# Two 3x3 convolution stages rewritten: strips of rows as 32x32 array tiles, a residual tap, statistics taken inside the stage

## The reference

```python
def _gn(v, G=16, eps=1e-5):
    ...
    m = jnp.mean(g, axis=(2, 3, 4), keepdims=True)
    s = jnp.var(g, axis=(2, 3, 4), keepdims=True)
    return ((g - m) / jnp.sqrt(s + eps)).reshape(v.shape)
...
# layer 1, first steps: 18 offset channels of which the kernel uses 10
offset = conv2d(input, offset_conv_w, offset_conv_b, padding=[(1, 1), (1, 1)])
offset = jnp.tanh(group_norm(offset, gn_offset_w, gn_offset_b, K))
...
# layer 2
out = jax.lax.conv_general_dilated(x, weight, ..., padding=((1, 1), (1, 1)))
return out + bias[None, :, None, None]
...
x = x + _L2_conv_ref(_gn(x), L2_conv_weight, L2_conv_bias)
x = x + _L3_conv_ref(_gn(x), ...)
```

## Time and profile before

| | |
|---|---|
| median of 3 runs | 25470.23 us (25365.6 to 25509.12) |
| profiled execution, first to last instruction | 25493.9 us |
| stage `l1o` in it (first transfer to the next stage's) | 797.4 us |
| stage `n1o` | 76.9 us |
| stage `l2` | 884.2 us |
| stage `n3` (to the first work of the next) | 125.9 us |
| TensorE busy in `l1o`, in `l2` | 365.4 us, 364.8 us |

### The profile page before, as it was taken

One profiled execution on the slowest core, in us unless ns is written; L12 is line 12 of the kernel. 1 busy time (PEld: TensorE's weight loads), 2 busy tenths in 40 slices (PEclk: granted clock), 3 DMA queues, 4 the chain that ended last, 5 costly groups with the idle time before them and its releaser, 6 DMA issues. The chain is left out here.

```text
span 25493.9 us, 384771 instructions
## 1 busy us (share of the span) xinstructions
PE 20717.4 (81%) x134800; PEld 8220.3 (32%) x134800; DVE 15361.5 (60%) x15737; ACT 14120.3 (55%) x22694; POOL 9395.5 (37%) x7816
## 2 busy tenths in 40 slices
PE   6888888884368888888859999997348888888899
PEld 2333333331122222222225444454013333333344
DVE  8999999994167777777835555555133333333111
ACT  6999998994257777777636665665222222222111
POOL 6777777782057777777720010001000000000000
PEclk9999999997678888888877776777679999999999
DMA  1000000006810000000031111112960011001111
GB/s 63 12 12 12 12 12 12 12 12 127 155 47 17 17 18 16 18 18 16 16 79 26 28 33 28 26 28 62 193 149 22 22 29 26 22 22 27 39 38 44
DMA packets 1295345, 995.42 MB, mean 39 GB/s; under 512 B 742248, under 2 KB 1151440, under 8 KB 1258968
## 3 DMA queue, kind: packets, MB, share of 16 engines
q1 hardware_dynamic: 1193416, 849.62, 15.9%
q0 software_dynamic: 26624, 100.67, 1.4%
q10 hardware_dynamic: 74448, 33.14, 0.5%
HBM read 771.60 MB, written 211.63 MB: 39 GB/s over the span
## 5 line engine op out<-in xcount | busy, mean ns | idle before, releaser
L270 DVE TENSOR_TENSOR l_mx<-l_p_v,l_puN 128x2048 f32<-128x2048 f32 x2560 | 5635.2, 2281 | 137.0 <-PE l_p_s L485 124.5
L485 PE MATMUL l_p_s<-l_mx,l_w2z 128*32 128x512 f32 x32768 | 3815.3, 610 | 579.5 <-ACT l_mx L397 307.9
L290 POOL TENSOR_TENSOR l_mx<-l_pv,l_puP 128x2048 f32<-128x2048 f32 x1024 | 3715.5, 3644 | 312.8 <-PE l_p_s L485 307.0
L1196 POOL TENSOR_TENSOR l1m_hc<-l1m_hs,l1m_cs 128x512 f32<-128x512 f32 x2304 | 2923.9, 1269 | 8.5 <-DVE l1m_hs L1148 8.1
L2072 PE MATMUL l3a_p<-l3a_xn,l3a_w 128*128 128x512 f32 (+1 forms) x6144 | 2682.9, 600 | 266.2 <-ACT l3a_xn L1963 266.2
L1148 DVE TENSOR_TENSOR_SCAN l1m_hs<-l1m_da,l1m_carry,l1m_pu 128x512 f32<-128x512 f32 x2304 | 2824.1, 1268 | 106.1 <-ACT l1m_da L1066 2.2
L2178 POOL DMA_DIRECT2D l3b_xt<-x_after x64 | 33.9, 529 | 7634.9 <-DVE l3b_most L2307 5811.9
L1790 ACT ACTIVATE l1d_ab<-l1d_pt 128x1024 f32<-128x1024 f32 x2304 | 2316.1, 1023 | 671.3 <-PE l1d_pt L1552 327.7
L416 ACT ACTIVATE l_mx<-l_pv,l_puP 128x128 f32<-128x128 f32 x8192 | 2446.7, 393 | 0.8
L1668 DVE TENSOR_SCALAR l1d_hat<-l1d_ab 128x1024 f32<-128x1024 f32 x2304 | 1917.0, 833 | 474.0 <-ACT l1d_ab L1790 363.6
L1587 PE MATMUL l1d_po<-l1d_hat,l1d_ring 128*32 128x128 f32 x36864 | 1893.2, 335 | 325.2 <-DVE l1d_hat L1668 214.1
(11 more groups left out here) (300 smaller groups left out, 27330.4 us busy)
## 6 DMA issues: line engine op xcount, KB each, us to landing
n_xt<-x_after SPq DMA_DIRECT2D x48, 2048.0 KB
l3a_xb<-x_after SPq DMA_DIRECT2D x352, 256.0 KB, 4.0
l1o_img<-x_after SPq DMA_DIRECT2D x32, 2032.0 KB, 17.5
l_img<-x_after SPq DMA_DIRECT2D x32, 2032.0 KB, 16.9
l1m_sq<-seq SPq DMA_DIRECT2D x256, 144.0 KB
n_xt<-in_x_dram SPq DMA_DIRECT2D x16, 2048.0 KB
l_xs<-in_x_dram SPq DMA_DIRECT2D x128, 256.0 KB, 2.8
x_after<-l_ot SPq DMA_DIRECT2D x128, 256.0 KB, 2.4
```

Source lines behind the costliest of these rows:

```text
L270: v.tensor_tensor(mx[:, r % QB, :, :, :], columns.unsqueeze(1).broadcast_to([P, 4, G, P]), rows.broadcast_to([P, 4, G, P]), ALU.max).then_ ...
L290: g.tensor_tensor(mx[:, r % QB, :, :, :], pv[:, u, :, :].unsqueeze(1).broadcast_to([P, 4, G, P]), rows.broadcast_to([P, 4, G, P]), ALU.add ...
L485: ins = pe.matmul(p_s[R * q:R * (q + 1), 512 * u:512 * (u + 1)], w2z[:, 31 - r:63 - r], mx[:, r % QB, q, :, :].rearrange("p t v -> p (t v) ...
L1196: g.tensor_tensor(hc[:, (3 * u + p) % 6, part, :], hs[:, p % 3, part, :], cs[:, u, :], ALU.mult).then_inc(hc_done, 1)
```

## The change

Both calls of `conv_layer` get a new body, and the two `norm_table` calls behind them (`n1o`, `n3`) go; the stage writes their tables itself. Lines L547 to L696 below are those of the changed kernel.

An image is cut into four strips of 32 rows. Strip s lies with its 32 channels in partitions 32 s to 32 s + 31 of `raw`, with one row more above and below, and is loaded once; the rows that belong to two strips are loaded twice. Loads go out on GpSimd's queue, stores on SyncE's. ScalarE normalises from `raw` into the padded `img` with one activation over 128 partitions and 4096 elements and four small ones for the border rows. A strip's 32 rows are four sub-strips k of 8 rows; a pass r (two for an image) makes four rows of each sub-strip. TensorE does, for each pass and each of nine taps, sixteen products, one on each 32x32 tile of the array: row tile s reads strip s, column tile k makes sub-strip k, and the result goes to bank 4 r + s. In `l2` a tenth tap with an identity matrix adds the unnormalised `raw`. An image takes 288 products in `l1o` and 320 in `l2`; the loop over images is written out for TensorE. ScalarE evacuates four banks at once with the bias. VectorE takes statistics of what was evacuated, and at the stage's end a product with `mean_strips` joins them over strips and channel pairs into the table. The scale and bias of all images are loaded once at the start.

```diff
--- before.py
+++ after.py
...
-def conv_layer(nc, stage, x, table, weights, bias, out, B, residual):
+def conv_layer(nc, stage, x, table, weights, bias, one, mix, out, out_table, B, residual):
...
+    S = 4
+    SR = H // S
+    SUB = SR // S
     RR = 512 // W
...
+    RN = SUB // RR
...
+        raw = m.sb("raw", [P, 2, SR + 2, W])
+        img = m.sb("img", [P, 2, SR + 2, WP])
...
+        ot = m.sb("ot", [P, 2, S, SUB, W])
...
+        acc = m.bank("acc", 2 * S)
...
+        @block.gpsimd
+        def _(g):
+            def load(b, u):
+                for s in range(S):
...
+                    g.dma_start(raw[strip(s), u, first:first + hi - lo, :],
+                                x[at(b), :, lo:hi, :].rearrange("b c h w -> (b c) h w")).then_inc(img_in[u], 16)
+            load(0, 0)
+            load(1, 1)
+            with g.Fori(0, B // 2 - 1) as j:
+                for u in range(2):
+                    g.wait_ge(norm_done, j * 2 + u + 1)
+                    if residual:
+                        g.wait_ge(conv_done, (j * 2 + u) * RN + 3 * RN)
+                    load(j * 2 + u + 2, u)
         @block.sync
         def _(sp):
...
+            tb = table.rearrange("b (c q) s -> c b q s", c=C)
+            for s in range(S):
+                sp.dma_start(gn[strip(s), :, :], tb[:, :, 0, :]).then_inc(w_in, 16)
...
+            for s in range(S):
...
             def store(b, u):
...
+                sp.wait_ge(evac_done, b * RN + 3 * RN)
+                for k in range(S):
+                    sp.dma_start(out[at(b)].rearrange("b c (s k r) w -> k (b c) s (r w)", s=S, k=S)[k],
+                                 ot[C * k:C * k + keep, u].rearrange("p s r w -> p s (r w)")).then_inc(stored[u], 16)
+            with sp.Fori(0, B // 2) as j:
                 for u in range(2):
                     store(j * 2 + u, u)
...
+            sp.wait_ge(tab_ready, 2)
+            sp.dma_start(out_table.rearrange("b (c q) s -> c b q s", q=q)[:, :, 0, :], tab[0:keep, :, :]).then_inc(tab_out, 16)
+            sp.wait_ge(tab_out, 16)
             for u in range(2):
                 sp.wait_ge(stored[u], (B // 2 + 1) * 64)
         @block.scalar
         def _(act):
...
+            act.wait_ge(w_in, 16 * n_w)
+            act.wait_ge(zeroed, 2)
+            def normalise(b, j, u):
+                act.wait_ge(img_in[u], j * 64 + 64)
+                act.wait_ge(conv_done, b * RN + RN)
+                def norm(part, rows):
+                    return act.activation(img[part, u, rows, 1:W + 1], raw[part, u, rows, :], ACT.Identity,
+                                          scale=gn[part, at(b), 0:1].rearrange("p b s -> p (b s)"), bias=gn[part, at(b), 1:2].rearrange("p b s -> p (b s)"))
+                norm(slice(C, 2 * C), slice(0, 1))
+                norm(slice(2 * C, P), slice(0, 1))
+                norm(slice(0, 2 * C), slice(SR + 1, SR + 2))
+                norm(slice(2 * C, 3 * C), slice(SR + 1, SR + 2))
+                norm(slice(0, P), slice(1, SR + 1)).then_inc(norm_done, 1)
+            def evacuate(b, j, u):
+                act.wait_ge(stored[u], j * 64 + 64)
+                act.wait_ge(stat_done, b * RN + RN)
+                for r in range(RN):
+                    act.wait_ge(conv_done, b * RN + (2 * RN + r + 1))
+                    act.activation(ot[:, u, :, RR * r:RR * (r + 1), :].rearrange("p s r w -> p s (r w)"),
+                                   acc[:, 512 * S * r:512 * S * (r + 1)].rearrange("p (s n) -> p s n", s=S),
+                                   ACT.Identity, bias=bc[:, 0:1]).then_inc(evac_done, 1)
+            normalise(0, 0, 0)
+            with act.Fori(0, B // 2 - 1) as j:
+                normalise(j * 2 + 1, j, 1)
+                evacuate(j * 2, j, 0)
+                normalise(j * 2 + 2, j + 1, 0)
+                evacuate(j * 2 + 1, j, 1)
+            normalise(B - 1, B // 2 - 1, 1)
+            evacuate(B - 2, B // 2 - 1, 0)
+            evacuate(B - 1, B // 2 - 1, 1)
...
         @block.tensor
         def _(pe):
...
+            pe.wait_ge(w_in, 16 * n_w)
+            taps = [(dy, dx) for dy in range(3) for dx in range(3)]
+            for j in range(B // 2):
                 for u in range(2):
...
+                    pe.wait_ge(norm_done, j * 2 + (u + 1))
+                    for r in range(RN):
+                        pe.wait_ge(evac_done, j * 2 * RN + (u * RN + r + RN + 1))
+                        for n, (dy, dx) in enumerate(taps):
+                            for s in range(S):
+                                for k in range(S):
+                                    r0 = SUB * k + RR * r + dy
+                                    ins = pe.matmul(acc[strip(k), 512 * (S * r + s):512 * (S * r + s + 1)], wt[strip(s), n, :],
+                                                    img[strip(s), u, r0:r0 + RR, dx:dx + W], start=n == 0,
+                                                    stop=n == len(taps) - 1 and not residual, tile_position=(C * s, C * k))
+                        if residual:
+                            for s in range(S):
+                                for k in range(S):
+                                    r0 = SUB * k + RR * r + 1
+                                    ins = pe.matmul(acc[strip(k), 512 * (S * r + s):512 * (S * r + s + 1)], idn[strip(s), :],
+                                                    raw[strip(s), u, r0:r0 + RR, :], start=False, stop=True, tile_position=(C * s, C * k))
                         ins.then_inc(conv_done, 1)
+            pe.wait_ge(mv_ready, 1)
+            pe.wait_ge(evac_done, B * RN + 2 * RN)
+            pe.matmul(acc[:, 0:2 * B], mx[:, :], mv[:, :, :].rearrange("p b s -> p (b s)"), start=True, stop=True).then_inc(mean_done, 1)
         @block.vector
         def _(v):
...
+                    for r in range(RN):
+                        v.wait_ge(evac_done, j * 2 * RN + (u * RN + r + 1 + 2 * RN))
+                        for s in range(S):
+                            ins = v.bn_stats(parts[:, at(j * 2 + u), S * r + s, :].rearrange("p b s -> p (b s)"),
+                                             ot[:, u, s, RR * r:RR * (r + 1), :].rearrange("p r w -> p (r w)"))
+                        ins.then_inc(stat_done, 1)
+            v.wait_ge(stat_done, B * RN + 2 * RN)
...
-    conv_layer(nc, "l1o", x1, tables[1], a["w_offset"], a["b_offset"], offsets, B, False)
-    norm_table(nc, "n1o", offsets, tables[2], a["pair_mean_half"], B)
+    conv_layer(nc, "l1o", x1, tables[1], a["w_offset"], a["b_offset"], a["one_strips"], a["mean_strips"], offsets, tables[2], B, False)
...
-    conv_layer(nc, "l2", x2, tables[3], a["w_l2"], a["b_l2"], x3, B, True)
+    conv_layer(nc, "l2", x2, tables[3], a["w_l2"], a["b_l2"], a["one_strips"], a["mean_strips"], x3, tables[4], B, True)
...
-    norm_table(nc, "n3", x3, tables[4], a["pair_mean"], B)
...
+def strip_conv(w):
...
+    o, i = w.shape[:2]
+    out = np.zeros((T, 9, T), np.float32)
+    out[:i, :, :o] = w.transpose(1, 2, 3, 0).reshape(i, 9, o)
+    return np.tile(out, (P // T, 1, 1))
...
+        mean_strips=np.tile(pair_means(2)[:T, :T], (P // T, P // T)) * (T / P), step_table=step_table, own_term=own_term, ident=one,
...
+        w_offset=strip_conv(I[L1 + "offset_conv_w"][:used]), b_offset=b_offset,
...
+        w_l2=strip_conv(I["L2_conv_weight"]), b_l2=I["L2_conv_bias"], b_conv1=I["L3_conv_conv1_b"],
```

More of the change, by code:

```diff
@@ L529, in _ @@
         @block.sync
         def _(sp):
[L531 to L547, removed]
@@ L549, in store @@
-            def store(b, u):
-                sp.wait_ge(evac_done, b * NS + 2 * NS)
-                for q in range(4):
-                    sp.dma_start(out[at(b), :, QR * q:QR * (q + 1), :].rearrange("b c h w -> (b c) (h w)"),
-                                 ot[C * q:C * q + keep, u, :]).then_inc(stored[u], 16)
-            load(0, 0)
-            load(1, 1)
-            with sp.Fori(0, B // 2 - 1) as j:
+            tb = table.rearrange("b (c q) s -> c b q s", c=C)
+            for s in range(S):
+                sp.dma_start(gn[strip(s), :, :], tb[:, :, 0, :]).then_inc(w_in, 16)
@@ L559, in _ @@
+            with sp.Fori(0, B // 2) as j:
                 for u in range(2):
                     store(j * 2 + u, u)
-                    load(j * 2 + u + 2, u)
-            for u in range(2):
-                store(B - 2 + u, u)
+            sp.wait_ge(tab_ready, 2)
+            sp.dma_start(out_table.rearrange("b (c q) s -> c b q s", q=q)[:, :, 0, :], tab[0:keep, :, :]).then_inc(tab_out, 16)
+            sp.wait_ge(tab_out, 16)
             for u in range(2):
@@ L607, in _ @@
-            v.memset(ot[:, 0, 2:3], 0.0).then_inc(stored[0], 64)
-            v.memset(ot[:, 1, 0:1], 0.0).then_inc(stored[1], 64)
-            v.wait_ge(w_in, 80)
+            for u in range(2):
+                v.memset(img[:, u], 0.0).then_inc(zeroed, 1)
+            v.memset(eps[:, :], EPS).then_inc(evac_done, 2 * RN)
+            v.memset(var[:, :], 0.0).then_inc(conv_done, 2 * RN)
```

(11 more changed lines are left out.)

92 lines of the change are left out of this document (41 added, 51 removed).

## The result

The changed kernel takes 24,515.8 us (median of 4 runs, 24,447.0 to 24,667.6) beside 25,468.9 us before (median of 4): 953 us less, and the two medians divide to 0.9626. The ratio on record, which goes by fast runs alone, is 0.9656, 95% interval 0.9612 to 0.9700, or 876 us. I had said 24,250 us and at most 24,520, against 25,470 a ratio of 0.952 and at most 0.963: the sign is right, the gain is about three quarters of the forecast, the median lies 4 us inside the end of the range, and the ratio on record just outside.

The account below looks back on a forecast made before the run. Transfers were taken to fill `l1o` and `l2`, slowed by using few partitions. New stages of 293 and 368 us sum to 661 against 1884.4, 1223 us less: 24,271 of 25493.9, adjusted to 24,250 us; range 24,120 to 24,520.

Parts of the forecast that it names:

- The feeding of TensorE: Both stages: sixteen pairs of weight load and pass issue in 0.43 us, 27 ns a pair, as a short run suggested.
- the rival that named it: Both stages: the sequencer sets the pace, up to 89 ns a pair, 2.85 us for sixteen products, total 25,400 us; chance 0.06.
- Sixteen products in 0.86 us: TensorE in both stages: two passes at 0.43 us; 15.5 us an image in `l1o`, 17.2 in `l2`.
- rows and columns overlap: TensorE in both stages: row and column tiles work at once, the lower bound of 0.86 us for sixteen products, against 3.44.
- row tiles in turn: Rival, both stages: row tiles take turns, sixteen products in 3.44 us, stages 2176 us, total 25,760 us; chance 0.05.
- half the rate: Rival, both stages: sixteen products in 1.72 us, by paired row tiles or low clock, total 24,715 us; chance 0.10.
- The chain of two images in `l2`: `l2`: load beside store, normalise, evacuation, products, hand-overs and clock follow each other, 41.0 us for two images, 20.5 an image.
- The start: Each stage: 15 us to the first normalisation, parameters and first load landing together, then 6.1 us to normalise.
- The end: Each stage: 3 us for the clock, 1.9 for the last evacuation, 17 for last statistics, table and barrier.
- Transfers: Both stages: a load takes 10.1 us and mostly overlaps stores, 11.7 us an image in `l1o`, 11.5 in `l2`.
- The tables: Separate stages `n1o` and `n3` go, saving 76.9 + 125.9 us; their statistics run beside other work.

Follow-up runs that it names:

- e5: Changed kernel with TensorE's loop body one image, passes making half the columns from padded buffers: `l1o` 370 us, `l2` 408 us, total 24,362 us.
- e2: Changed kernel loading only the first two images, the other fourteen reusing their strips: `l1o` 375 us, `l2` 402 us, total 24,288 us.
- e4: Changed kernel with row strips multiplied one after the other, four column tiles at a time: `l1o` 1583 us, `l2` 1701 us, total 26,815 us.
- e9: One-image loop with parameters first, each product on 256 columns for 512, half the output rows left out: `l1o` 263 us, `l2` 285 us, total 23,961 us.
- e3: Changed kernel with each strip loaded in pieces of at most 9 rows, packets of 4.6 KB: `l1o` 431 us, `l2` 473 us, total 24,546 us.
- e6: One-image loop, with GpSimd waiting for the stage's parameters before loading the first image: `l1o` 362 us, `l2` 402 us, total 24,298 us.
- e1: Changed kernel with TensorE's written-out stream made a loop over pairs of images: `l1o` 521 us, `l2` 521 us, total 24,843 us.

## Why the prediction was right in sign and wrong in size

The stages were to take 661 us and take 941.5; the difference is made of these (with e5's images as those without a fetch; e5 differs in its passes and hand-overs too, so the two middle rows are good to some us):

| us | `l1o` | `l2` |
|---|---|---|
| start, first transfer to first pass: 21.1 forecast | +10.8 | +10.7 |
| sixteen products at 1.06 us and hand-overs, e5's images against 249.6 and 324.7 | +72.8 | +35.3 |
| instruction fetch, the changed kernel's images against e5's | +105.8 | +57.6 |
| end: 21.9 forecast, 15.7 and 16.4 measured | -6.2 | -5.5 |

**The feeding of TensorE was the step that failed.** The prediction asked for a pair of weight load and pass every 27 ns, said that "no row shows that pace for 576 pairs of an image", and put nothing for the fetch into its sum; the rival that named it was priced as an even pace, at 0.06. It cost 163 us of the 281 that were missing, and not as an even pace: calm stretches run at 33 ns a pair, and then the stream stops for 1 to 6.6 us, because a packet of 128 pairs comes late while an image is loaded (e2, e4, e5). The number of instructions was in the change, 288 or 320 products written out for 16 images; that a loop of the kernel before fetches nothing was to be seen in its queue of instructions, 3 packets in a stage, and I had not read that row. The Trainium skill ("Runtime: NRT & Kernel Launch", section "Instruction fetch mechanics") says that TensorE's instruction memory holds 2048 instructions and is refilled in blocks of 16 KiB. The trace agrees: packets of 1.18 MB / 72, bodies of 1160 and 1288 weight loads and passes that stay, and one of 2320 that doesn't. It also says that crossing a block is mostly hidden, and that a taken branch to a target outside the current two pages has to fetch it. Here the packets cost 163 us in two stages, and a loop of one image, some five packets long, took 4 or 5 packets in 16 turns. The measurement decides.

**Sixteen products in 0.86 us** was mis-sized: 1.06, 2 x (0.43 + 0.10). The row was there: a pass on four row tiles at 0.53. I put the difference down to a first weight load and took the column tiles' 0.43. In `l1o` this is 57 of the 73 us in the table's second row (16 x 18 x 0.197), and most of the rest is the first image, 28.4 us in e5 for 19.7 later. In `l2` the forecast's 20.5 us an image had covered most of it, since a chain of waits was to be longer than the products. That rows and columns overlap held: sixteen tiles cost what four row tiles cost, so "row tiles in turn" and "half the rate" are out. The Trainium skill ("TensorE: Matmul & The Clock Gate", section "The mechanism") says that a weight load overlaps with running products only where the row group differs. The sixteen tiles, with all rows in use, agree by the size of what is added (0.10 us, e9); the column tiles of the earlier trace rows and of e4, on the same rows and with nothing added, do not.

**The chain of two images in `l2`** (41.0 us, 20.5 an image) never ended last. The waits in `l2`:

```profile
ACT l_img L603 <- DMA l_raw<-x_after: 172.9, 14, 12.5
...
PE l_acc L647 <- ACT l_img L603: 42.3, 1, 42.3
```

ScalarE does wait for loads there, but TensorE waits for ScalarE only at the start, and from the second image on starts an image 4.7 us or more after it is normalised: at 21.2 us of products, and 26.1 with the pauses, it is behind the chain anyway. So the order was right, load after the last product, and the term was hidden behind one that I had too small.

**The start** was forecast 11 us too short, because the small rows of scale and bias stand behind 17 KB packets of two images (e3: first pass at +20.9 with small packets; e6: +24.7 with the parameters ahead). **The end** cost 6 us less: 3 of its 21.9 were for the clock, which is lost elsewhere, and the table of `l1o` landed 2.5 us after its issue, where the earlier trace rows gave 7.2. That this hides half of the start's error is chance. **Transfers** went as taken: the load lands in 9.9 to 12.2 us by the page's issues, and they overlap, since e9 moves an image's loads and stores in 13.8 and 15.2 us, and one behind the other they were to take 20.5 and 19.7. The tables gave their full 203 us.

That the other 740 us came at all is the transfers': TensorE's work on an image stayed what it was, 20.6 us before by the prediction's passes, 19.7 and 21.8 plus the pauses now, while transfers fell from filling the stages (117 MB in `l1o`) to 0.6 of them (53 MB).

## What to carry to other kernels

Count the instructions of a stream that is written out, and look at the profile's queue of instructions: a stage that took a packet for every 4 us of TensorE's work stopped here whenever transfers were dense, and a loop whose body stays (1288 weight loads and passes here) removed this, for a rearrangement of buffers and 35 us more work on ScalarE, which had it to spare. Price a round on four row tiles by its columns plus 0.10 us, not by columns alone. When transfers stop being the bound, price the next engine from the row that resembles the new shape most, even if a smaller figure stands beside it.

## What the runs showed of the hardware

- Instruction packets of 16 KB start mostly 3.4 to 4.2 us apart in calm stretches of TensorE's stream in `l2`, and 6.8 to 8.7 us apart beside an image's load, though each takes 0.9 to 1.4 us once it has started; neither packets of 4.6 KB nor a quarter of the bytes in flight took the pauses away. Why they start late stays open.
- A loop body of 1160 or 1288 weight loads and passes took 4 and 5 instruction packets in 16 turns (e5), one of 2320 took 86 in 8 (e1).
- With four 32x32 tiles at work the granted clock stayed at 0.50 (1.2 GHz) through stages of 1583 and 1701 us in which TensorE was busy 97% of the time (e4); in the stages with sixteen it is 0.84 to 0.94.
- Sixteen passes, one on each 32x32 tile, take their columns' time and some 0.10 us that doesn't depend on columns (e9), about a weight load (0.104 us). Four on one row tile take the columns' time alone (e4). Where the 0.10 comes from is not shown.
